# Sorting the tokens of a mixture of experts by expert group into 19 tiles of eight experts

## The chip, the cores and the metric

The kernel runs on one core of one Trainium2 chip, as one launch. The metric is the device time of that launch in microseconds, from timed executions; one further execution was profiled. The engines named below are PE (the matrix engine TensorE), VectorE (DVE), ScalarE (ACT), GpSimd (POOL) and SyncE (SP), which issues most DMAs.

## What is computed

The input is x, 4 sequences of 1024 tokens of 256 numbers. Two blocks follow one another, each `x + attention(norm(x)) * silu(ffn(norm(x)))`. The change touches the first block. Its FFN, cut to what matters:

```python
sb = sigmoid(x @ gate_w.T) + gate_bias                # 32 experts in 4 groups of 8
_, gidx = top_k(sum of the two best of each group, 2) # 2 groups of each token
_, topi = top_k(masked to these two groups, 8)        # 8 experts of 16
cw[token, topi] = wsel / wsel.sum() * 2.5             # weights, zero elsewhere
x_lat = x @ fc1_w.T                                   # 256 -> 128
h = relu(einsum('tl,eil->eti', x_lat, w1)) ** 2       # 128 -> 128 per expert
y_lat = einsum('eti,eli->tl', h * cw, w2)             # 128 -> 128, summed over experts
out = relu(x @ shared_up_w.T) ** 2 @ shared_down_w.T + y_lat @ fc2_w.T
```

The attention beside it has 16 heads of 16 and LoRA-extended projections; its q, k and v are computed in the same stage as the FFN.

## The kernel before

The 4096 tokens are cut into 8 chunks of 512 (`CH`). The kernel has four stages, each with its own blocks of instructions for the five engines: `first_half` (norm, q, k, v, the whole FFN of block 1), `first_attention`, `gate_network` (the FFN of block 2) and the second attention. Within a stage each engine walks through one list of steps, made by `first_half_plan` or `first_attention_plan`, and does its own part of each. So the list sets the order of the work on every engine, SP's DMA issues among them, and each engine is strictly in order. `Psum` hands out the eight banks of PSUM to the steps: PE waits in `P.all_before(s)` until the bank's last user is through.

In `first_half` a chunk goes through these steps. `load` and `sums`, `begin`: x is loaded and normed. `turn`: PE turns it, ScalarE writes the high part `xh`, VectorE the low part `xl`; products of such pairs are three products (`mm3`, lines 104 to 109). `gate`, `gate_turn`, `latent`: scores and the 128 latent numbers of a token. `groups`, `chosen`, `eight`, `weigh`: VectorE picks groups and experts with some fifty small instructions and writes the weights `cw`. `qk`, `values`, `shared`: projections; q, k, v are stored to DRAM (`qk_rest`, `values` on SP). Then all 32 experts on all 512 tokens: `up` (PE, three products of 512 columns; ScalarE: relu in line 490, square into `sq` in line 496), `down` (PE, line 596, two passes for each of four groups of 128 tokens), and VectorE adds the product times `cw[:, i, e]` to the sum `y` (line 797). The tail of a chunk is `tail_turn` (the sum is turned), `mix` (shared `sdn` and routed `fc2` products into one bank) and a sigmoid and product that leave silu(ffn) in `M["g"]`. It runs while the next chunk's experts do. While the experts of chunk c run, the steps of chunk c+1 up to `shared` are slipped in between.

Near the end `ahead` loads the q and k of the first two units of the attention, and 19 `max` steps (`BEGUN`) are done ahead: two score products of 512 columns in a pair of banks, and one VectorE reduction over both (line 176). 13 of them stand between the experts of the last chunk, six between the parts of its tail. `rows` turns the finished maxima, and `store_rows` writes them by four DMAs into the rows that the first score product reads.

In `first_attention` a step pair is one `max`, one pair of score products (line 1043), two exponentials on ScalarE (line 1007) and the product with the values (line 1056, `pv`). 256 steps `i` with two halves each make up the stage. The `max` steps keep ahead of the scores and take two pairs of banks in turn. `weights` steps (`GATE`) quantize the weights of the next stage.

Of the kernel before, what the change touches and what calls it, by code (L numbers as in the profile page):

```python
# [10 lines left out]
ALU = mybir.AluOpType  # L11
# [14 lines left out]
ACT_TURNS = (0, 1, 2, 3)  # L26
# [191 lines left out]

def first_half_plan():

    p = [("load", 0), ("weights",), ("load", 1), ("sums", 0), ("begin", 0), ("w_first",)]
    p += [("w_lora", n, k) for n in range(4) for k in range(2)]
    p += [("turn", 0, 0), ("turn", 0, 1), ("gate", 0), ("latent", 0), ("gate_turn", 0), ("groups", 0),
          ("w_shared",), ("w_experts", 0), ("shared", 0, 0), ("chosen", 0), ("shared", 0, 1), ("eight", 0),
          ("shared", 0, 2), ("weigh", 0), ("shared", 0, 3), ("qk", 0, 0), ("qk", 0, 1), ("qk_rest", 0, 0)]
    begun = {0: [("values", 0, 0)], 1: [("qk_rest", 0, 1), ("qk", 0, 2)], 2: [("values", 0, 1), ("w_experts", 1)],
             3: [("qk_rest", 0, 2), ("qk", 0, 3)], 5: [("qk_rest", 0, 3)], 10: [("w_experts", 2)],
             18: [("w_experts", 3)]}
    plan = {0: [("sums",)], 2: [("begin",)], 4: [("turn", 0)], 5: [("turn", 1)], 6: [("gate",)], 7: [("latent",)],
            8: [("gate_turn",)], 9: [("groups",)], 10: [("qk", 0)], 12: [("qk_rest", 0), ("chosen",)],  # L230
            13: [("qk", 1)], 15: [("qk_rest", 1), ("eight",)], 16: [("qk", 2)], 18: [("qk_rest", 2), ("weigh",)],
            19: [("qk", 3)], 20: [("values", 0)], 21: [("qk_rest", 3)], 22: [("shared", 0)], 24: [("shared", 1)],
            26: [("shared", 2)], 28: [("values", 1)], 30: [("shared", 3)]}

    begin = range(7, E, 2)
    tail = {1: [("tail_turn",)], 3: [("mix", 0)], 5: [("mix", 1)]}
    for c in range(NCH):
        if c + 2 < NCH:
            p.append(("load", c + 2))
        p += [("up", c, 0), ("up", c, 1)]  # L240
        for e in range(E):
            if c:
                p += [(s[0], c - 1, *s[1:]) for s in tail.get(e, [])]
                if c == NCH - 1 and e in (6, 16):
                    p.append(("ahead", e // 16))
            else:
                p += begun.get(e, [])
            if c + 1 < NCH:
                p += [(s[0], c + 1, *s[1:]) for s in plan.get(e, [])]
            if e + 2 < E:  # L250
                p.append(("up", c, e + 2))
            if c == NCH - 1 and e in begin:
                p.append(("max", begin.index(e)))
            p.append(("down", c, e))
    last = NCH - 1

    def maximum(n):
        x = len(begin) + n
        return [("max", x), ("both", 0)] if x == 15 else [("max", x)]

    p += [("mix_up", last, 0, 0)] + maximum(0)
    p += [("tail_turn", last)] + maximum(1)
    p += [("mix_up", last, 0, 1), ("mix_end", last, 0)] + maximum(2)
    p += [("mix", last, 0), ("mix_up", last, 1, 0)] + maximum(3)
    p += [("rows", 0)] + maximum(4)
    p += [("mix_up", last, 1, 1)] + maximum(5)
    return p + [("mix_end", last, 1), ("mix", last, 1)]

def first_half(nc, block, A, M, X):  # L270
    with ExitStack() as ctx:
# [7 lines left out]
        xh = [M["xh"][:, :, i * CH:(i + 1) * CH] for i in range(2)]  # L279
        xl = [M["xl"][:, :, i * CH:(i + 1) * CH] for i in range(2)]  # L280
        aa = [sb(f"aa{i}", [128, 2, CH], FR) for i in range(2)]
        va = sb("va_", [128, 2, H0, 32])
        lh = [sb(f"xlh{i}", [128, CH], FR) for i in range(2)]
        ll = [sb(f"xll{i}", [128, CH], FR) for i in range(2)]
        scT = sb("scT", [E, CH])
        sc = sb("sc", [128, 4, E])
        cw = [sb(f"cw{i}", [128, 4, E]) for i in range(2)]
        g = {k: sb(k, s) for k, s in dict(
            sb_=[128, 4, E], m8=[128, 16, 8], gs=[128, 4, 4], cc=[128, 4, 6], wn=[128, 4, 4], sel=[128, 4, 4],
            nb=[128, 4, 4], mk=[128, 4, E], mk2=[128, 4, E], t8=[128, 4, 8], rp=[128, 4, E], tk=[128, 4, E],  # L290
            ww=[128, 4, E], sm=[128, 4], rc=[128, 4]).items()}
        rl = M["rl"]
        sq = [sb(f"sq{i}", [128, CH]) for i in range(4)]
        hs = [sb(f"hs{i}", [128, 4, CH]) for i in range(2)]
        y = [sb(f"yac{i}", [128, 4, 128]) for i in range(2)]
        yT = sb("yT", [128, CH])
        sg = sb("sg", [128, 2, 256])
        bk = sb("bk", [128, 2, 2])
        x_t = A["x"].rearrange("(c i p) d -> c p i d", i=4, p=128)

        lora = hs[1]
        r_qkv = [t[:, :, :].rearrange("p a b -> p (a b)").rearrange("p (c o) -> p c o", c=2) for t in y]
        r_qkv.append(sq[3][:, :].rearrange("p (c o) -> p c o", c=2))
        r_f = yT[:, 0:320].rearrange("p (c o) -> p c o", c=2)
        r_s = hs[0][:, 0:2, :]
        r_1 = [hs[i][:, j:j + 2, :].rearrange("p a b -> p (a b)").rearrange("p (e o) -> p e o", e=8)
               for i, j in ((0, 2), (1, 0), (1, 2), (1, 0))]
        folded = r_qkv + [M["wo"]]

        plan = first_half_plan()
        P = M["banks"].stage()
        small = n_max = 0
# [1887 lines left out]
```

## Time and profile before

| | us |
|---|---|
| timed executions, median of 3 | 3142.89 |
| lowest, highest | 3141.05, 3150.26 |
| the profiled execution, its own time | 3153.16 |
| its span, first to last instruction | 3151.3 |

| busy in the profiled span | us | share |
|---|---|---|
| PE | 3018.0 | 96% |
| VectorE | 2118.1 | 67% |
| ScalarE | 1862.7 | 59% |
| GpSimd | 1013.5 | 32% |

The profile gives for each engine its busy time; for groups of instructions their number, busy time and mean duration; and for idle time of an engine what ended it. PE's matmuls overlap: the duration of one is longer than the distance to the next, so the distance between two starts is what one costs. A matmul of plain float32 appears as two. The clock that PE was granted is either full (1.0) or half (0.5) in any stretch. The first score product of the attention starts at 678.85 us, and the attention's last product at 1457.25 us.

### The profile page before, as it was taken

Reading aid. Unit: us, or ns where it says so; the run is one execution under the profiler, and the core shown is the slowest. Engines: PE = TensorE matmul, PEld = TensorE weight load, DVE = VectorE, ACT = ScalarE, POOL = GpSimd, SP = SyncE. Lnnn points to the kernel's source line nnn. Section 1 sums busy time; section 2 is a strip of 40 time slices with the busy share of each in tenths; the row PEclk is TensorE's granted clock in tenths of the full one; section 3 lists DMA queues with packets and bytes.
Section 4 is the critical chain, followed back from the end, with each engine's and each line's share of the span. In section 5 each row is a group of like instructions: output and inputs, shape, how many; then the busy total and the mean of one; then the engine's idle time right before and its main releaser. Section 6 shows DMA issues by size and latency. Waiting matters only on the chain. (4 is left out here: it accounts for less than half of the span.)

```text
span 3151.3 us, 66387 instructions
## 1 busy us (share of the span) xinstructions
PE 3018.0 (96%) x23638; PEld 2264.8 (72%) x23638; DVE 2118.1 (67%) x5888; ACT 1862.7 (59%) x4638; POOL 1013.5 (32%) x1627
## 2 busy tenths in 40 slices
PE   7999999999999999997988999999999999999999
PEld 5888888853444444444877888788887888788887
DVE  5666666678999989984755555655556555565556
ACT  4666666647877777774445555455554555545553
POOL 0000000001100000001016566576655766566653
PEclk9999999988999999998999999999999999999999
DMA  4111111231332232202324434354343543344431
GB/s 150 48 48 48 48 48 41 61 69 31 81 48 55 46 73 35 42 4 89 115 59 111 104 94 99 96 128 103 84 117 87 119 103 93 93 115 110 97 89 44
DMA packets 296483, 246.35 MB, mean 78 GB/s; under 512 B 148956, under 2 KB 231516, under 8 KB 296028
## 3 DMA queue, kind: packets, MB, share of 16 engines
q1 hardware_dynamic: 296156, 242.11, 31.2%
q8 instruction: 191, 3.13, 0.4%
q14 instruction: 136, 1.11, 0.1%
HBM read 100.71 MB, written 44.04 MB: 46 GB/s over the span
## 5 line engine op out<-in xcount | busy, mean ns | idle before, releaser
L1853 ACT ACTIVATE b_pp<-b_pp,b_nm 128x192 f32<-128x192 f32 (+2 forms) x1024 | 472.9, 463 | 452.8 <-DVE b_nm L2020 371.3
L176 DVE TENSOR_REDUCE mx<-ps 128x2 f32<-128x1024 f32 x512 | 622.4, 1224 | 64.4 <-PE ps L167 51.9
L1007 ACT ACTIVATE a_pt<-ps 128x512 f32<-128x512 f32 x1024 | 555.9, 595 | 185.3 <-PE ps L1043 184.3
L1823 POOL TENSOR_SCALAR b_pp<-b_pp,b_rc 128x192 f32<-128x192 f32 x960 | 387.0, 425 | 384.8 <-DVE b_rc L2029 384.8
L2041 DVE COPY b_pt<-ps 128x384 f32<-128x384 f32 (+2 forms) x336 | 181.9, 555 | 317.1 <-PE ps L1942 301.8
L2020 DVE CUSTOM_DVE_ANT_0 b_pp<-ps,b_mk 128x192 f32<-128x192 f32 x960 | 276.3, 353 | 134.9 <-PE ps L1921 134.9
L797 DVE SCALAR_TENSOR_TENSOR f_yac<-ps,f_cw,f_yac 128x128 f32<-128x128 f32 x992 | 277.9, 343 | 125.4 <-PE ps L596 123.0
L596 PEld LDWEIGHTS ps<-w,f_sq 128*128 128x128 f32 x2048 | 265.1, 191 | 26.5 <-issue 6.0
L596 PE MATMUL ps<-w,f_sq 128*128 128x128 f32 x2048 | 270.1, 275 | 0.3
L1976 PE MATMUL ps<-b_wo,b_oT 128*128 128x256 f32 x1024 | 241.6, 380 | 3.7 <-ACT b_vv L1846 3.7
L1056 PE MATMUL ps<-a_pt,a_v 128*32 128x256 f32 x3072 | 242.9, 396 | 0.0
L1942 PE MATMUL ps<-ident,b_pp 128*128 128x128 f32 x1440 | 234.2, 273 | 2.7 <-DVE b_qp L1998 2.5
L990 POOL TENSOR_TENSOR a_s<-a_s,g 128x256 f32<-128x256 f32 x32 | 23.4, 730 | 573.9 <-DVE a_s L1114 573.9
L1921 PE MATMUL ps<-b_kp,b_qp 64*128 64x192 f32 x1920 | 189.9, 337 | 18.0 <-ACT b_vv L1846 10.2
L1976 PEld LDWEIGHTS ps<-b_wo,b_oT 128*128 128x128 f32 x1024 | 185.3, 190 | 25.3 <-ACT b_vv L1846 4.4
L1942 PEld LDWEIGHTS ps<-ident,b_pp 128*128 128x128 f32 x1440 | 177.8, 141 | 34.2 <-issue 3.7
L490 ACT ACTIVATE rl<-ps 128x512 f32<-128x512 f32 x256 | 151.7, 593 | 80.0 <-PE ps L109 75.5
L1846 ACT ACTIVATE b_vv<-ps 128x256 f32<-128x256 f32 x256 | 97.5, 381 | 169.1 <-PE ps L109 168.8
L1921 PEld LDWEIGHTS ps<-b_kp,b_qp 64*128 64x128 f32 x1920 | 154.7, 188 | 56.3 <-issue 56.3
L1995 DVE TENSOR_TENSOR b_qf<-ps,xt 128x512 f32<-128x512 f32 x256 | 174.2, 681 | 29.5 <-PE ps L109 29.5
L1853 ACT ACTIVATION_READ_ACCUMULATOR b_pp<-b_pp,b_nm 128x1 f32 x1024 | 191.3, 187 | 0.0
L1968 PE MATMUL ps<-b_pt,b_vv 128*64 128x128 f32 x960 | 189.6, 279 | 0.0
(282 smaller groups left out, 7335.9 us busy)
## 6 DMA issues: line engine op xcount, KB each, us to landing
b_rt<-b_qf SPq DMA_DIRECT2D x1024, 64.0 KB, 2.0
qk_parts<-f_aa SPq DMA_DIRECT2D x32, 512.0 KB, 2.7
v_rows<-f_va_ SPq DMA_DIRECT2D x16, 512.0 KB, 2.8
rl<-in_W1qT SPq DMA_DIRECT2D x64, 128.0 KB, 2.6
rl<-in_W1kT SPq DMA_DIRECT2D x64, 128.0 KB, 2.6
rl<-in_W1vT SPq DMA_DIRECT2D x32, 256.0 KB, 3.0
b_wo<-in_W1oT SPq DMA_DIRECT2D x16, 512.0 KB, 3.7
b_vs<-b_vv SPq DMA_DIRECT2D x60, 128.0 KB, 2.9
```

What stands on the lines that cost most here:

```text
L176: e.tensor_reduce(M["mx"][kh % 3][:, :, jt, h], P.pair(s), AX.X, ALU.max, negate=True).then_inc(P.free_sem(s), 1)
L596: m = e.matmul(P.ap(s)[:, i * 128:(i + 1) * 128], sq[d % 4][:, i * 128:(i + 1) * 128], M["w2"][:, s[2], :], start=True, stop=True)
L797: m = e.scalar_tensor_tensor(out=o, in0=src, scalar=by, in1=o, op0=ALU.mult, op1=ALU.add)
L1007: e.activation(pt[(4 * i + 2 * j + a) % 12][:, :], P.ap((*s, a)), ACT.Exp).then_inc(P.free_sem((*s, a)), 1)
L1056: m = e.matmul(P.ap(group)[32 * j:32 * j + 32, x], vs[b % 2][c][:, 4 * g + j, :], pt[(4 * i + j) % 12][:, x], start=c == half == 0, stop=c ...
L1823: m = e.tensor_scalar(x, x, r[:, 2 * u + h:2 * u + h + 1], 1.0, ALU.mult, ALU.mult)
L1853: e.activation(x, x, ACT.Exp, bias=nm[n % 4][:, c:c + 1], scale=-1.0, accum_out=sm[n % 4][:, c:c + 1]).then_inc(exp_done, 1)
L1921: m = e.matmul(scores(u, h), q[r, d:d + 128], kk[r, d:d + 192], start=True, stop=True)
L1942: m = e.transpose(P.ap(f)[:, c * 128:(c + 1) * 128], pp[n % 3][:, at:at + 128], ident[:, :])
L1968: e.matmul(o1, v[:, i + u, right + 64:right + 128], y[:, 2, :], start=u == 0, stop=False)
L1976: m = e.matmul(P.ap(s)[:, 0:256], oT[:, n % 2 * 4 + c, t * 128:(t + 1) * 128], wo[n % 2][:, c, :], start=c == 0, stop=c == 3)
L2020: m = e.tensor_tensor_reduce(out=weights(n, u, h), in0=scores(u, h), in1=mask, scale=-0.125, scalar=3e38, op0=ALU.add, op1=ALU.min, accum_ ...
```

## The change

Instead of running all 32 experts on all tokens, each token is copied once for each of its two groups into a slot of a table in DRAM, sorted by group; each group starts at a multiple of 512 slots. 8192 pairs of token and group then fill at most 19 tiles of 512 slots, and a tile is run through the eight experts of one group. Weights of a slot are those eight entries of `cw`, carried behind the 128 latent numbers (`SW` = 136).

- Phase one, eight chunks: `turn`, then four `row` steps, each one product of 128 tokens with v, fc1 and gate beside one another (416 columns). ScalarE takes sigmoid and latent copy from it, VectorE the values. `begin` moves from VectorE to GpSimd. The routing steps stay on VectorE and gain instructions that count (`one1`, `total`); `rank` counts with products of a triangular matrix the place of each token in its group. `qk`, `shared`, `sdn` are put into a list `behind` and dealt out as `quota`; up to six chunks of `xh`, `xl` are kept for this (`RING`).
- At the start SP writes zeros over the whole slot table, ahead of the load of chunk 1. The folds of v come before those of q, k and o.
- `places` computes the position of each pair and the group of each tile. 64 indirect DMAs on GpSimd (`scatter`) write the rows to their slots. 42 pieces of `behind` stand after it for PE.
- Phase two, 19 tiles: `w_load` loads the group's weights (1 MB, address from a register), `w_split` splits them (ScalarE, GpSimd), `slots` loads the rows, `lat` turns them, then `up` and `down` for eight experts, and `y_out` stores the sums. The maxima stand in the last four tiles (16) and behind them (3), all in one pair of banks.
- The routed tail moves into the attention, chunk c at steps 8c+8 to 8c+15: `gather` (eight indirect DMAs), `add`, `tail_turn`, `mix` (fc2, added to the shared part in `M["g"]`), `ex` (max, exp, +1) and `silu` (reciprocal on VectorE, product on GpSimd). The `weights` steps move from step 16 to step 84.
The diff, cut to its core:

```diff
 def first_half_plan():
-    p = [("load", 0), ("weights",), ("load", 1), ("sums", 0), ("begin", 0), ("w_first",)]
+    p = [("load", 0), ("weights",), ("load", 1), ("sums", 0), ("begin", 0)]
+    p += [("w_lora", 2, k) for k in range(2)] + [("w_first",), ("turn", 0, 0), ("turn", 0, 1), ("sums", 1), ("begin", 1)]
+    p += [("w_lora", n, k) for n in (0, 1) for k in range(2)]
...
+    c = NCH - 1
+    p += [("groups", c)] + quota(1) + [("chosen", c)] + quota(1) + [("eight", c)] + quota(1) + [("weigh", c)]
+    p += quota(1) + [("rank", c)] + quota(1) + [("places",)]
+    p += [("scatter", n) for n in range(32)] + [("w_load", m) for m in range(1)]
+    while behind:
+        p += quota(1)
+    p += [("slots", 0), ("w_split", 0), ("w_load", 1), ("slots", 1), ("lat", 0)]
+    for m in range(NT):
+        p += [("up", m, 0), ("up", m, 1)]
+        for e in range(NE):
+            if m + 1 < NT and e == 1:
+                p.append(("w_split", m + 1))
+            if m + 1 < NT and e == 3:
+                p.append(("lat", m + 1))
+            if e + 2 < NE:
+                p.append(("up", m, e + 2))
+            if m < 2 and e == 0:
+                p.append(("ahead", m))
+            if m >= NT - 4 and e % 2:
+                p.append(("max", (m - NT + 4) * 4 + e // 2))
...
+            p.append(("down", m, e))
+            if e == NE - 1:
+                p.append(("y_out", m))
+                if m + 2 < NT:
+                    p += [("w_load", m + 2), ("slots", m + 2)]
+    return p + [("max", 16), ("max", 17), ("rows", 0), ("max", 18)]
...
+                    for i in range(4):
+                        n = NT * GT // 4
+                        e.dma_start(X["slots"][i * n:(i + 1) * n, :].rearrange("(p r) d -> p r d", p=128),
+                                    spread(zero[:, :], 1, n // 128)).then_inc(zero_out, 16)
...
+                elif k == "w_load":
+                    w.wait_ge(pos_ready, 3)
+                    if c == 1:
+                        w.wait_ge(*P.filled(("sdn", NCH - 2, 1)))
+                    if c >= 2:
+                        w.wait_ge(*P.filled(("down", c - 2, NE - 1)))
+                    group = e.value_load(tile_of[0:1, c:c + 1], min_val=0, max_val=NG - 1)
+                    e.dma_start(raw[c % 2][:, :, :].rearrange("p e f -> p (e f)"),
+                                A["w12"][bass.ds(group, 1), :, :].rearrange("a p f -> p (a f)")).then_inc(raw_in[c % 2], 16)
...
+                elif k == "y_out":
+                    w.wait_ge(*P.emptied(("down", c, NE - 1)))
+                    e.dma_start(X["y"][c * GT:(c + 1) * GT, :].rearrange("(i p) d -> p i d", p=128),
+                                y[c % 2]).then_inc(y_out[c % 2], 16)
...
+                elif k == "scatter":
+                    w.wait_ge(picked, 2 * NCH)
+                    w.wait_ge(row_act, 4 * NCH)
+                    w.wait_ge(zero_out, 64)
+                    w.wait_ge(pos_ready, 2)
+                    for i in range(2):
+                        e.indirect_dma_start(X["slots"], bass.IndirectOffsetOnAxis(ap=M["pos"][:, i, c:c + 1], axis=0),
+                                             rows[:, c, i, :], None).then_inc(row_out, 16)
+                elif k == "w_split":
+                    w.wait_ge(e_high, c + 1)
+                    if c >= 2:
+                        w.wait_ge(*P.filled(("up", c - 2, NE - 1)))
+                    e.tensor_tensor(w1[1][c % 2], raw[c % 2][:, :, 0:128], w1[0][c % 2].bitcast(F32),
+                                    ALU.subtract).then_inc(e_low, 1)
...
+                elif k == "w_split":
+                    w.wait_ge(raw_in[c % 2], 16 * (c // 2 + 1))
...
+                    e.activation(w1[0][c % 2], raw[c % 2][:, :, 0:128], ACT.Copy).then_inc(e_high, 1)
...
+                elif k == "row":
...
+                    for j in range(2):
+                        m = mm3(e, P.ap(s)[:, 0:416], xh[c % RING][:, j, t], xl[c % RING][:, j, t],
+                                M["wr_h"][:, j, :], M["wr_l"][:, j, :], j == 0, j == 1)
+                    m.then_inc(P.full_sem(s), 1)
...
 def first_attention_plan():
...
+        if 8 <= i < 8 * NCH + 8:
+            x, k = i // 8 - 1, i % 8
+            if k == 0:
+                p.append(("add", x))
+                if x + 1 < NCH:
+                    p.append(("gather", x + 1))
+            elif k == 2:
+                p.append(("tail_turn", x))
+            elif k in (3, 4):
+                p.append(("mix", x, k - 3))
+            elif k == 5:
+                p += [("ex", x, y) for y in range(2)]
+            elif k == 7:
+                p += [("silu", x, y) for y in range(2)]
...
+                elif k == "silu":
+                    w.wait_ge(up_one, 2 * s[1] + n + 1)
+                    e.reciprocal(ex[n], ex[n]).then_inc(inverted, 1)
```

## Rows read from the trace of the kernel before

**Rows 1.** Cores: span and mean granted clock; page, part 1: busy time.

```profile
core 0: 3151.3 us, clock 0.985
PE 3018.0 (96%) x23638; PEld 2264.8 (72%) x23638; DVE 2118.1 (67%) x5888; ACT 1862.7 (59%) x4638; POOL 1013.5 (32%) x1627
```

**Rows 2.** Timeline of PE in chunk 1: start, duration, engine, line, operation, count.

```profile
204.71 0.60 PE L602 MATMUL ps<-ident,f_yac 128*128 128x128 f32 x4
205.06 0.48 PE L107 MATMUL ps<-f_xlh,w_h 128*128 128x512 f32 x1
...
206.65 0.48 PE L107 MATMUL ps<-f_xlh,w_h 128*128 128x512 f32 x1
...
208.33 1.89 PE L534 MATMUL ps<-sdn,f_hs 128*128 128x256 f32 x8
210.06 0.59 PE L539 MATMUL ps<-fc,f_yT 128*128 128x256 f32 x2
```

**Rows 3.** Timeline of PE: first gate product, and two products of 256 columns.

```profile
27.00 0.77 PE L107 MATMUL ps<-xh,wg_h 128*128 128x512 f32 x1 [1.61 <-DVE xl L693]
...
49.29 0.28 PE L107 MATMUL ps<-wqkv_h,xh 128*128 128x256 f32 x1
49.41 0.28 PE L108 MATMUL ps<-wqkv_l,xh 128*128 128x256 f32 x1
```

**Rows 4.** DMA issues, size and time to landing, of 14:16, 22:32, and the page.

```profile
xt<-in_x SPq DMA_DIRECT2D x1, 512.0 KB, 11.8
...
f_hs<-in_w1T SPq DMA_DIRECT2D x2, 512.0 KB, 4.5
...
b_rt<-b_qf SPq DMA_DIRECT2D x1024, 64.0 KB, 2.0
```

**Rows 5.** Groups by line (busy, mean ns, idle before); last, an SP issue.

```profile
L496 ACT ACTIVATE f_sq<-rl 128x512 f32<-128x512 f32 x250 | 158.0, 632 | 8.0
L490 ACT ACTIVATE rl<-ps 128x512 f32<-128x512 f32 x251 | 148.7, 593 | 78.8 <-PE ps L109 74.3
...
L434 ACT ACTIVATE w1b_h<-f_hs 128x1024 fp32r<-128x1024 f32 x2 | 2.1, 1042 | 0.0
...
L990 POOL TENSOR_TENSOR a_s<-a_s,g 128x256 f32<-128x256 f32 x32 | 23.4, 730 | 573.9 <-DVE a_s L1114 573.9
...
0.74 0.44 SPq L362 DMA_DIRECT2D xt<-in_x  x1
```

**Rows 6.** Timeline of PE at the crossing into the attention.

```profile
678.85 0.49 PE L1043 MATMUL ps<-xh,xl 50*128 50x512 f32 x2 [0.96 <-DMA xh<-n]
681.46 0.79 PE L1043 MATMUL ps<-xh,xl 50*128 50x512 f32 x2 [2.11 <-ACT a_pt L1007]
```

**Rows 7.** Busy time by stretch: PE, PEld, DVE, ACT, POOL, granted clock, DMA.

```profile
678.85:732.00 53.15, 50.05 (x269) 17.44 (x269) 32.91 (x30) 27.66 (x50) 0.29 (x3) 0.52 0.22 51
732.00:784.00 52.00, 48.38 (x449) 20.88 (x449) 47.44 (x47) 41.95 (x78) 11.33 (x5) 0.99 0.24 46
```

**Rows 8.** Groups by line and form: VectorE's reciprocals.

```profile
L2029 DVE RECIPROCAL b_rc<-b_sm 128x8 f32<-128x8 f32 x120 | 23.0, 192 | 0.0
...
L1101 DVE RECIPROCAL a_rc<-ps 128x16 f32<-128x16 f32 x32 | 8.2, 257 | 20.2 <-PE ps L1066 19.7
...
L2029 DVE RECIPROCAL b_rc<-b_sm 128x2 f32<-128x2 f32 x32 | 5.0, 155 | 0.2 <-ACT b_pp L1853 0.2
```

**Rows 9.** Page, part 5: the maxima on VectorE.

```profile
L176 DVE TENSOR_REDUCE mx<-ps 128x2 f32<-128x1024 f32 x512 | 622.4, 1224 | 64.4 <-PE ps L167 51.9
```

**Rows 10.** Timeline of PE in the attention around a second low spell.

```profile
782.84 0.50 PE L167 MATMUL ps<-w1b_l,w1b_h 48*128 48x512 f32 x2 [0.85 <-DVE mx L176]
...
784.66 0.79 PE L167 MATMUL ps<-w1b_l,w1b_h 48*128 48x512 f32 x2
...
786.79 0.50 PE L167 MATMUL ps<-w1b_l,w1b_h 48*128 48x512 f32 x2
...
788.03 0.50 PE L167 MATMUL ps<-w1b_l,w1b_h 48*128 48x512 f32 x2
```

More of the change, by code:

```diff
@@ L25 @@
 NTURN = B * NP
-ACT_TURNS = (0, 1, 2, 3)
+GT, SW = 512, 136
 class Waits:
@@ L216, in store_rows @@
                         M["n2"][n % 2][8 * a:8 * a + 8, r, :].bitcast(F32)).then_inc(M["rows_in"][i][h], 16)
+NG = 4
+NT = 19
+NE = E // NG
+RING = 6
 def first_half_plan():
-    p = [("load", 0), ("weights",), ("load", 1), ("sums", 0), ("begin", 0), ("w_first",)]
[L222 to L233, printed above, removed]
@@ L238, in first_half_plan, with quota @@
+    behind += [[("sdn", NCH - 1, j // 2, j % 2)] for j in range(4)]
+    def quota(n):
+        out = []
+        for s in behind[:n]:
+            out += s
+        del behind[:n]
+        return out
+    for c in range(NCH):
+        if c:
+            p += [("turn", c, 0), ("turn", c, 1)]
         if c + 2 < NCH:
             p.append(("load", c + 2))
[L240 to L267, printed above, removed]
+        if c and c + 1 < NCH:
+            p += [("sums", c + 1), ("begin", c + 1)]
@@ new lines, in first_half_plan @@
+        if c == 0:
+            p += [("row", 0, 0), ("row", 0, 1), ("val", 0, 0), ("row", 0, 2), ("val", 0, 1), ("row", 0, 3),
+                  ("val", 0, 2), ("w_shared",), ("val", 0, 3)]
+            p += [("w_lora", 3, k) for k in range(2)]
+            continue
+        p += [("groups", c - 1)] + quota(1)
+        p += [("row", c, 0), ("chosen", c - 1), ("row", c, 1), ("val", c, 0)] + quota(1)
+        p += [("eight", c - 1), ("row", c, 2), ("val", c, 1)] + quota(1)
+        p += [("weigh", c - 1), ("row", c, 3), ("val", c, 2)] + quota(1)
@@ L312, in first_half @@
         P = M["banks"].stage()
-        small = n_max = 0
-        in_chunk = sum(s[0] == "max" for s in plan[:plan.index(("down", NCH - 1, E - 1))])
+        n_small = n_b = n_max = 0
+        begun = sum(s[0] == "max" for s in plan)
         for s in plan:
             if s[0] == "max":
-                x = 6 * (n_max % 2) if s[1] >= in_chunk else 0
-                P.take(s, x, x + 1)
-                n_max += 1
-            elif s[0] == "rows":
-                P.take(s, 4)
-            elif s[0] == "mix_up":
-                if s[3] == 0:
-                    P.take(("mix", *s[1:3]), 2 + s[2])
-            elif s[0] in ("tail_turn", "mix") and s[1] == NCH - 1:
-                if s[0] == "tail_turn":
-                    P.take(s, 5)
-            elif s[0] in ("w_lora", "turn", "gate", "gate_turn", "latent", "qk", "values", "shared", "tail_turn", "mix"):
-                P.take(s, small % 3)
-                small += 1
+                P.take(s, 0, 1)
+            elif s[0] in ("w_lora", "turn", "row", "rank"):
+                P.take(s, n_small % 4)
+                n_small += 1
+            elif s[0] == "places":
+                P.take(s, n_small % 4)
+                n_small += 1
+            elif s[0] in ("qk", "shared"):
+                P.take(s, 4 + n_b % 3)
+                n_b += 1
+            elif s[0] == "sdn" and s[3] == 0:
+                P.take(("sdn", *s[1:3]), 7)
+            elif s[0] in ("lat", "rows"):
+                P.take(s, 2)
@@ L346, in first_half @@
         y_done, dve_done = sem("y"), sem("dve")
-        LOW = {"gate": 1, "latent": 2, "bias": 3, "q": 5, "k": 7, "v": 9, "shared": 10, "experts": 11}
+        LOW = {"v": 2, "f": 3, "g": 4, "bias": 5, "q": 7, "k": 9, "shared": 10}
         def x_is_used(c):
-            return P.filled(("shared", c, 3) if c else ("qk", 0, 3))
+            return P.filled(last_use[c])
         def sync(e):
@@ L903, in first_attention @@
                 last = 0
-            elif s[0] in ("rows", "one", "two", "three") or s[:2] == ("weights", "sum"):
+            elif s[0] in ("rows", "one", "two", "three", "tail_turn", "mix") or s[:2] == ("weights", "sum"):
                 if last is None:
```

642 lines of the change are left out of this document (397 added, 245 removed).

## The prediction

> **What bounds the kernel now.** I read the page first. PE is busy for 96% of the span and the granted clock is 0.985 on average [rows 1]: time goes down only if PE has less to do, and goes up wherever PE is made to wait. Then the PE timeline inside a chunk of the first half [rows 2]. One expert on 512 tokens is a pitch of 1.59 us (205.06 to 206.65), three products of 512 columns and eight narrow passes, with no idle between. The reader is to see that this pitch stands 256 times (8 chunks x 32 experts), 407 us of the 679 us before the attention [rows 6]. Last, the attention: PE 48.4 and VectorE 47.4 busy of 52 us [rows 7]. Two engines are nearly full there, and a double maximum keeps VectorE for 1.23 us [rows 9].
>
> **Experts.** 19 tiles x 8 experts replace 256 units by 152: 104 x 1.59 = 165.4 us less of PE, all on the path. This is the only large gain.
>
> **Token rows.** Gate, latent and values (12 products of 512 columns and 24 of 256 a chunk; one of 256 takes 0.12 us [rows 3], so one of 512 some 0.23; with four small turns 5.8 us) become 24 products of 416 columns at 0.19 us, 4.5 us. Eight chunks: -9 us. The routed tail (four turns in 0.35 us; four fc2 products, of the form of the four sdn products that have a pitch of 1.73 us; 2.1 us a chunk [rows 2]) leaves the first half: -17 us here; its return is priced below.
>
> **Tile overhead.** 19 `lat` turns at 0.35 us, and 19 starts instead of 8 where PE waits some 0.25 us for the first square: +10 us.
>
> **Start.** The zero fill of the slot tensor (9728 rows of 544 B, 5.3 MB, four DMAs) is put on SP ahead of the load of chunk 1. Before, that load, issued between 14 and 16 us, landed 11.8 us later [rows 4], behind some 3.9 MB; 4.3 MB in 12 to 15.5 us is 0.28 to 0.36 MB/us. Now 7 MB lie there (the 2.5 MB of expert weights are gone): 20 to 25 us, landing near 36 us. VectorE has `sums` 1 ahead of the folds of q and k, those hold the small banks, and `row` 0 wants them: PE waits for this load. First token product near 39 us instead of 27.00 us [rows 3]; the earlier fold of v buys nothing. Since less PE work lies ahead of that point than before, I take +9 us; bounds -10 (the fill does not delay the load) to +15.
>
> **Scatter.** After `places`, PE has 42 pieces of `behind` left: 12 qk and 13 shared at 1.4 us, 17 sdn at 1.73 us [rows 2], 64 us. Against this stand about 3 us of small VectorE steps, 64 indirect DMAs on POOL, a landing of 2.0 us [rows 4], the load of `slots` (2.8 us), turns and splits (2 us). The trace shows no indirect DMA. Below: the issue of a plain one, 0.44 us [rows 5], 28 us in all, hidden. Above: each waiting for its own landing, 2.0 us, 128 us, 74 exposed. I take the sum of that issue and one 0.73 us POOL pass [rows 5], 1.2 us: 77 us, so 23 us exposed, and 3 us for a clock that then starts low: +26 us, bounds 0 to +77.
> The Trainium skill (DMA: Bandwidth & Descriptors, Anatomy of one DMA, SWDGE path) calls descriptor generation small and lays the 2 us on the completion; by it the scatter would be hidden and the sum 26 us lower. No row here shows it.
>
> **Weights of a tile.** `w_load` m+2 stands on SP behind `y_out` m, which waits for VectorE's last accumulation of tile m (1.35 us after its last product T). With the issue, a register load and the next issue it leaves at T+2.7; 1 MB was two 512 KB loads landing in 4.5 us [rows 4]: T+7.3. ScalarE meets its `w_split` in the next tile after three expert units, at T+4.2, and blocks. Behind it stand a copy of 1024 columns (1.04 us) and five units of 1.23 us (0.593 + 0.632) with the `lat` copy [rows 5]: the last `down` ends 9 us after the landing, T+16.4, where PE alone needs 13.1. That is 3.3 us for 14 tiles and 1 us for the three that also hold maxima: +49 us, bounds 25 (landing 1.4 us sooner) to 60. Each tile then has a hole of 2.6 us; if the clock falls in it, up to 2.6 us more a tile; I take 10 us, bounds 0 to 44. The split's POOL part (about 2.6 us) is hidden in the rest of the tile, and so are the slot loads. Cover gone, each costs its length.
>
> **Crossing to the attention.** Before, PE idled 0.96 and 2.11 us there and the clock fell [rows 6]. Now only four maxima and a turn lie between the last `down` and the first score, which waits for `rows` and its four DMAs: about +3.5 us. The 19 maxima themselves are the same number.
>
> **The tail inside the attention.** Per chunk PE gets 2.1 us, POOL and ScalarE short steps and eight gathers, which their idle time hides. VectorE gets two PSUM adds (1.4 us) and two reciprocals of 128x512. Reciprocals of 2, 8 and 16 columns took 155, 192 and 257 ns [rows 8]: 6.2 to 8.1 ns a column, not the one-a-cycle of a plain step. So 3.3 to 4.3 us each; I take 3.8, 7.6 us in one block. Only two maxima's banks lie ahead of PE, so PE stands about 6 us in each block. That is a hole larger than those after which the clock fell before: 0.85 us idle was followed by one short low spell, the crossing by one of about 51 us [rows 6, 10]. At the low level the pitch of the steps was 2.13 us (784.66 to 786.79), at the high one 1.24 [rows 10]. Per chunk: 6.2 (hole) + 2.1 + 6 (some seven slots at the low level, 0.89 us each) = 14.3, eight chunks: +114 us. Bounds: +55 (VectorE's 9 us a chunk less its 2 us slack, clock never lost) to +200 (low throughout: 16 x 0.89 + 4.2 + 6 a chunk).
> The Trainium skill (VectorE: DVE Perf Modes, First, the fixed hardware budget) says that reciprocal is an iterated divide with a repeat count of 8; at that page's 0.96 GHz that is, as an estimate, 4.3 us a tile and about 8 us more in all. The rows agree in kind.
>
> **Sum.** -165 - 9 - 17 + 10 + 9 + 26 + 49 + 10 + 3.5 + 114 = +30 us. The profiled execution took 3153.2 us (span 3151.3), the median of the timed runs is 3142.9; nothing after the first attention is touched, so the same 30 us go on the median: 3173 us.
>
> **Rivals.**
> 1. The clock comes back at once and the holes are all that is paid: tail +60 instead of +114, no low clock in the tiles. Then -34, 3109 us. For it: the spell at 783 us was short [rows 10]. Against: the 51 us spell came with PE fully busy [rows 7].
> 2. Reciprocals run near a column a cycle and the fixed part grows instead: tail +30, 3089 us. Against: three sizes in a line [rows 8].
> 3. Transfers are quicker than I say: scatter hidden, `w_load` in time: 26 + 59 less, 3088 us. It decides at 1 us an indirect DMA and a landing at T+4.2; the 4.5 us of [rows 4] speak against.
> 4. The clock stays low through the eight chunks: +200 instead of +114, 3259 us; it decides where holes recur sooner than the clock returns (hole each 30 to 40 us, spell 51 us).
> 5. The sort doesn't do what it says: 19 tiles hold any split of 8192 pairs into four groups, so the units are 152 whatever the data; this falls away.
>
> **How the numbers follow.** Forecast 0.42 (own range 3145 to 3215), rival 1 0.22, rival 2 0.08, rival 3 0.13, rival 4 0.15. Likeliest: 3173 us. Range for 8 in 10: 3075 to 3255. A measurement can tell about 0.3%, 9.4 us. Slower: 0.38 of the forecast, all of rival 4, little of rival 1: 0.56. Same: 0.10. Faster: 0.34.
>
> **What the profile would show.** `f_sq` products x1216 (two passes each of 608) instead of x2048. First token product near 39 us, else the start is wrong. The last scatter's end on POOL against the last sdn product; idle of PE there near 23 us. In tiles 1 to 17 a pitch of 16 us with an idle of ScalarE released by the raw load; 13 us if wrong. Reciprocals of 128x512 on VectorE at 3 to 4.5 us, each pair followed by an idle of PE put down to `mx`, and a granted clock well under 1 for the first eight half units of the attention. A reciprocal under 1 us or a clock at 1.0 there would make the prediction wrong by the most.

## The result, and the profile after

The kernel after took 3269.7 us (3263.9 to 3275.0), the kernel before 3142.0 us in the same job: a ratio of 1.040, 95% interval 1.037 to 1.044. It is slower, and 97 us over the 3173 us forecast. The unchanged kernel after was run in two more jobs (a job is one sitting on one chip, with runs of the kernel before between): 3264.7 us in one, 3201.5 us in the other, while the kernel before stayed at 3140 to 3143. So there are two numbers to explain: +59 us, which it cost in the second of these, and +64 us more, which it cost in the others.

The cores and part 1 of the page of the kernel after, which answer to [rows 1]:

```profile
core 0: 3273.2 us, clock 0.949
...
PE 2950.1 (90%) x22524; PEld 2154.9 (66%) x22524; DVE 2051.8 (63%) x5496; ACT 1767.8 (54%) x4528; POOL 1314.0 (40%) x1912
```

PE is busy 68 us less than before, and the span is 122 us longer: PE's idle time grew by 190 us. Where, is seen from three points. The last product of the last `down` starts at 664.6 us (before: 663.6), the first score at 674.9 (678.85, [rows 6]), the last one at 1557.8 (1441.4). Before the attention the kernel gained 4 us instead of the 84 of the sum; the attention grew by 120 us, where the sum had 114; behind it 5 us were added.

**The scatter.** Busy time by stretch (PE, PEld, DVE, ACT, POOL, granted clock, DMA), and below it ScalarE's timeline in the same stretch, then PE's and GpSimd's:

```profile
190.00:230.00 40.00, 18.95 (x82) 14.94 (x80) 3.12 (x5) 7.31 (x12) 30.05 (x32) 0.79 0.39 131
230.00:275.00 45.00, 12.58 (x34) 9.02 (x34) 0.75 (x1) 2.51 (x4) 31.54 (x33) 0.58 0.19 65
```

```profile
214.76 0.69 ACT L584 ACTIVATE f_aa<-ps,bqk 128x512 fp32r<-128x512 f32 x1 [5.83 <-remote]
233.66 0.60 ACT L600 ACTIVATE g<-ps 128x512 f32<-128x512 f32 x1 [18.21 <-remote]
250.46 0.60 ACT L590 ACTIVATE f_rl<-ps 128x512 f32<-128x512 f32 x1 [16.20 <-remote]
...
267.26 0.69 ACT L584 ACTIVATE f_aa<-ps,bqk 128x512 fp32r<-128x512 f32 x1 [15.54 <-issue]
280.61 0.60 ACT L590 ACTIVATE f_rl<-ps 128x512 f32<-128x512 f32 x1 [12.66 <-remote]
```

```profile
204.06 1.89 PE L706 MATMUL ps<-sdn,f_hs 128*128 128x256 f32 x8
...
251.86 3.75 PE L706 MATMUL ps<-sdn,f_hs 128*128 128x256 f32 x8 [41.87 <-issue]
```

```profile
205.94 0.96 POOL L535 DMA_INDIRECT slot_rows<-f_rows,pos  x1 [0.31 <-issue]
```

PE works for 31.5 of 85 us, though 64 us of pieces stand ready. ScalarE copies the sdn product of 204.06 only at 233.66, 28 us after PE's last pass of it, and its wait ends on a semaphore event ("remote") with no instruction near it. The trace also holds the moment of each increment: those of PE's banks come singly at 207.65, 214.74, 233.64 and 250.44, and then four within 0.25 us, from 280.59 to 280.83, seven us after the end of the last indirect DMA (273.5). The products were done, their increments were not out. (ScalarE's start at 267.26, 17 us after the one before, has no increment of PE beside it in the trace.) VectorE's and ScalarE's own increments came at once. GpSimd issues an indirect DMA every 1.26 us all that time.

**A tile.** SP's queue, then the wait that it ends on ScalarE and on PE, around 400 us:

```profile
395.45 0.35 SPq L453 DMA_DIRECT2D f_hs<-in_w  x1
395.85 0.43 SPq L460 DMA_DIRECT2D f_rows<-slot_rows  x1
```

```profile
401.45 1.06 ACT L608 ACTIVATE w1b_h<-f_hs 128x1024 fp32r<-128x1024 f32 x1 [4.01 <-DMA f_hs<-in_w]
```

```profile
402.27 0.66 PE L713 MATMUL ps<-ident,f_rows 128*128 128x128 f32 x4 [2.67 <-DMA f_rows<-slot_rows]
```

The weights land 6.0 us after their issue and ScalarE stands 4.0 us for them; PE stands 2.7 us at `lat`, for the slot load that was issued behind them.

**The attention.** VectorE, and PE behind it:

```profile
777.83 6.55 DVE L1308 RECIPROCAL a_raw<-a_raw 128x512 f32<-128x512 f32 x2
```

```profile
785.52 0.79 PE L167 MATMUL ps<-w1b_l,w1b_h 48*128 48x512 f32 x2 [4.99 <-DVE mx L176]
```

One reciprocal of 512 columns takes 3.3 us; each pair leaves PE idle for 5 us, and a spell of the low clock (783.5, for 20.5 us) begins in that hole. Behind the first spell of 51 us stand 13 more before the last score, 3 to 20 us long; in the kernel before, one of 3 us did.

### The profile page after: what moved, and what is told of

Read it like the earlier page. It is cut to its first block and busy times, and to the rows that moved or that the text cites. A ratio compares the mean times of both kernels' runs of the same rounds, so it can differ in the third digit from the quotient of the medians.

```text
span 3273.2 us, 63773 instructions
## 1 busy us (share of the span) xinstructions
PE 2950.1 (90%) x22524; PEld 2154.9 (66%) x22524; DVE 2051.8 (63%) x5496; ACT 1767.8 (54%) x4528; POOL 1314.0 (40%) x1912
## 5 line engine op out<-in xcount | busy, mean ns | idle before, releaser
L2184 PE MATMUL ps<-b_pt,b_vs 128*64 128x128 f32 x960 | 190.4, 280 | 0.0
L2186 PE MATMUL ps<-b_pt,b_vb 128*64 128x128 f32 x960 | 184.1, 274 | 0.0
L2187 PE MATMUL ps<-b_pt,b_vb 128*64 128x128 f32 x960 | 184.1, 274 | 0.0
L941 DVE SCALAR_TENSOR_TENSOR rl<-ps,f_rows,rl 128x128 f32<-128x128 f32 x532 | 147.3, 345 | 34.5 <-PE ps L724 34.1
```

What stands on the lines that cost most here:

```text
L2184: e.matmul(o0, vs[x][:, i + u, :], y[:, 0, :], start=u == 0, stop=False)
L2186: e.matmul(o0, vb[x][:, i + u, 0:64], y[:, 1, :], start=False, stop=u == 3)
```

## The experiments

The stages of every kernel, in us of its profiled execution; the first tile begins with its `lat`, and the pitch is an eighteenth of the time from there to the last product of the 19th `lat`. "Attention" runs from the first to the last score. The kernel before took 3140 to 3144 us in every job (median).

| kernel | job | first tile | pitch | first score | attention | time |
|---|---|---|---|---|---|---|
| before | | | | 678.9 | 762.5 | 3142 |
| after | 1 | 319.9 | 17.73 | 674.9 | 882.9 | 3269.7 |
| e1, plain passes | 2 | 284.0 | 17.43 | 633.5 | 869.6 | 3211.5 |
| e2, paced | 2 | 277.6 | 17.65 | 630.8 | 861.2 | 3202.9 |
| e3, three buffers | 2 | 278.6 | 14.14 | 567.5 | 848.6 | 3141.6 |
| e4, power on GpSimd | 2 | 278.6 | 17.61 | 631.9 | 2032.8 | 4377.8 |
| e5, after again | 3 | 278.4 | 17.08 | 621.6 | 860.4 | 3201.5 |
| e6, zero later | 3 | 259.5 | 17.36 | 607.6 | 865.2 | 3186.1 |
| e7, sigmoid | 3 | 278.5 | 17.59 | 631.1 | 842.5 | 3183.4 |
| e8, three fixes | 3 | 259.7 | 14.13 | 548.3 | 831.9 | 3097.6 |
| e9, no tail | 4 | 320.4 | 17.40 | 669.3 | 759.1 | 3146.2 |
| e10, exp and ln | 4 | 321.5 | 17.75 | 676.9 | 912.1 | 3295.1 |
| e11, three, ln | 4 | 302.6 | 14.28 | 593.9 | 908.4 | 3218.9 |
| e12, after, third | 4 | 321.6 | 17.55 | 673.3 | 869.1 | 3264.7 |
| e13, passes again | 5 | 282.8 | 17.24 | 629.2 | 878.8 | 3232.7 |
| e14, paced again | 5 | 287.7 | 17.81 | 644.1 | 881.3 | 3249.6 |
| e15, tanh | 5 | 321.1 | 17.41 | 670.2 | 844.4 | 3228.0 |
| e16, three, tanh | 5 | 301.8 | 14.14 | 590.6 | 842.6 | 3147.9 |
| e17, tanh, spread | 6 | 277.7 | 17.16 | 622.4 | 787.1 | 3125.0 |
| e18, all, paced | 6 | 259.3 | 14.12 | 547.8 | 784.1 | 3044.2 |

**What holds the increments back.** e1 and e13 put a plain pass in the place of each indirect DMA:

```diff
-                        e.indirect_dma_start(X["slots"], bass.IndirectOffsetOnAxis(ap=M["pos"][:, i, c:c + 1], axis=0),
-                                             rows[:, c, i, :], None).then_inc(row_out, 16)
+                        w.wait_ge(row_out, 16 * (2 * c + i))
+                        e.tensor_tensor(flat[:, 1024:1536], flat[:, 0:512], flat[:, 512:1024],
+                                        ALU.subtract).then_inc(row_out, 16)
```

> The 64 indirect DMAs of the scatter become 64 plain passes of 512 columns on GpSimd (about 1.3 us each, so GpSimd is busy as long as before); the rows are not put into the slot tensor, so the routed part of the output is left out. Theory A (the issue of indirect DMAs is what keeps TensorE's semaphore increments back): the 42 pieces run at their own pace between 190 and about 256 us, TensorE's idle there falls from over 50 us to about 20 (waiting for GpSimd at the end), the first tile starts near 282 instead of 318 us, time 30 to 40 us under the kernel after. Rival B (the stores of q and k, the 1 MB weight load or the sheer length of the GpSimd work stop ScalarE): the steps of about 17 us stay, less than 8 us gained.

PE's stall in the scatter was gone, but it was also gone from the three other kernels of that job, which kept their indirect DMAs. So e1 told nothing, and the kernel after had to be run again.

> The kernel after, unchanged, a second time. In its first trace TensorE stood 42 us between 209.6 and 251.9 us while its semaphore increments arrived in steps of about 17 us; four other kernels, one of which differs only inside the attention, issued the same 64 indirect DMAs without that stall, and their first tile started at 278 us against 320. Theory D (the stall belongs to this build and comes each time): 3262 to 3277 us again, the first tile near 320 us, increments in steps. Theory E (the stall was an event of that chip or of those executions): the first tile at 278 us and 3222 to 3238 us.

> The kernel after, unchanged, a third time, for how often its executions show the stall of 42 us in the scatter. Theory E (an event of single executions or one chip): first tile at 278 us and 3195 to 3225 us. Theory D (it belongs to the build): 3262 to 3277 us.

No stall in e5, the same stall in e12. The build is not its cause, and within a job it was there in every profiled execution with the 64 DMAs in a row, or in none. The test had to be made in a job that shows it, and job 5 did (e15: PE busy 19.2 us of the 40 from 190 to 230, first tile at 321.1; e16, whose scatter begins 18 us sooner: first tile at 301.8).

> The kernel of e1 (64 plain GpSimd passes of 512 columns in place of the 64 indirect DMAs; the routed part of the output is left out) a second time, beside kernels with the scatter in the same job. If the others of this job show the stall of 42 us (first tile near 320 us): theory A (it needs the indirect DMAs) gives a first tile at 284 us here and no held increments; theory B (it belongs to the chip or the rest of the program) a first tile near 320 us. If the others show no stall, this run decides nothing.

The stretches of e13, in that job:

```profile
190.00:230.00 40.00, 39.90 (x175) 32.79 (x176) 7.29 (x10) 18.31 (x29) 35.99 (x29) 1.00 0.40 142
230.00:275.00 45.00, 20.98 (x93) 16.89 (x91) 2.25 (x3) 10.32 (x16) 40.42 (x33) 0.79 0.10 38
```

GpSimd is busier than in the kernel after, the plain loads and stores are those of the kernel after, and PE never waits until its pieces end. The gathers in the attention, eight indirect DMAs in a row, are left in e13, and there PE does stand in the same execution, behind the row from 779.4 to 788.3 us for instance:

```profile
791.57 0.50 PE L167 MATMUL ps<-w1b_l,w1b_h 48*128 48x512 f32 x2 [2.56 <-ACT spare L1202]
```

Theory A holds: the stall needs the indirect DMAs. Whether their issue or their transfers hold the increments is not told apart, since e13 has neither. What differs between jobs stays open too; the five jobs of the experiments ran on five chips, so it can be the chip or the moment.

**Pacing them.** e2 and e14 put a `scatter` step behind each piece, and GpSimd waits for a product first:

```diff
+            p.append(("scatter", n, next((t for t in p[::-1] if t[0] in ("qk", "shared")))))
...
+                    w.wait_ge(*P.filled(s[2]))
```

> GpSimd issues two indirect DMAs and then waits for the next product of the pieces behind, instead of 64 in one go. Theory A with increments that pass as soon as GpSimd pauses: products and pairs interleave at about 2.5 us a pair, 32 pairs and the ten pieces left end near 290 to 295 us, so the tiles start 20 to 25 us sooner and the time is that much under the kernel after. Theory A' (each increment is held until some 6 us after GpSimd's last issue, as the burst of four at 280.6 us suggests): every pair costs about 9 us, 32 pairs 290 us, the time is 130 to 180 us over the kernel after. Rival B: no change within 8 us.

> The kernel of e2 (two indirect DMAs after each product of the pieces) a second time. In a job with the stall: theory A gives a first tile before 300 us if increments pass as soon as GpSimd waits, and far behind 320 us if each is held some 6 us after the last issue. In a job without it: 278 us as before.

In the quiet job it changed nothing at the first tile (277.6). In the job with the stall the first tile came at 287.7 instead of 321: theory A, not A'. The waits work only once PE is behind. From 190.8 to 223.6 us GpSimd still issued 26 in a row and PE stood once for 20.2 us; at its first pause, from 223.6 to 228.0, three increments came through. The time fell by less than the stage: 17 us under the mean of 3267 us for the kernel after in jobs 1 and 4, in another job.

**The tiles.**

```diff
-                if m + 2 < NT:
-                    p += [("w_load", m + 2), ("slots", m + 2)]
+                if m + 3 < NT:
+                    p += [("w_load", m + 3), ("slots", m + 3)]
```

(with a third buffer for each in the space of `rows`, and the waits and semaphores by 3).

> Three buffers instead of two for a tile's weights and for its slots, so that both loads leave a whole tile sooner. Theory (the tiles wait for these two loads): the pitch of a tile falls from 17.7 us to 13.7 to 14 us, the low clock in the tiles goes with it, 60 to 75 us under the kernel after. Rival (the split of the weights on ScalarE and GpSimd or VectorE's accumulation is late next): a pitch of 16 us or more, less than 30 us gained.

The pitch fell to 14.14 us, a little over the 13.7 to 14 expected: no wait of PE on a load is left between the first tile and the last. Its wait on VectorE's accumulation stays, this in each tile:

```profile
380.56 1.16 PE L727 MATMUL ps<-f_raw,f_rows 128*128 128x128 f32 x8 [0.33 <-DVE rl L944]
```

So VectorE is next, but for 0.3 us. From first tile to last `down` it is 278.5 us instead of the 332.9 us of e5: 54 us. The time fell by 60 us against e5, another job, and by 61 us against e2 in its own. Both loads were moved at once, so what the weights and what the slots cost is not told apart.

**The start.**

```diff
+        if 1 <= c <= 4:
+            p.append(("zero", c - 1))
...
+                elif k == "zero":
                     w.wait_ge(pool_set, 1)
-                    for i in range(4):
+                    for i in (c,):
```

> The four DMAs that zero the slot tensor leave the start and stand one each behind the loads of chunks 3 to 6. Theory (the load of chunk 1 waits behind the fill on the same rings): the first token product comes at 27 to 31 us instead of 40, and nothing else moves: 8 to 12 us under whatever the kernel after shows in the same job. Rival (the start waits for the weights and the folds, not for the fill): first token product at 38 us or later, less than 3 us.

The first token product in PE's timeline of e6:

```profile
21.37 0.72 PE L107 MATMUL ps<-wr_h,xh 128*128 128x416 f32 x1 [2.73 <-DVE f_rows L777]
```

That line stood at 39.48 us in e5, with an idle of 20.73 before it. The first tile came 18.9 us sooner, the time fell by 15 us, more than the 8 to 12 expected.

**The tail in the attention.** e9 leaves it out.

> The kernel after without the tail in the attention: gathers, sum, turns, fc2 products, exponential, reciprocal and product are left out (the routed part and the silu are missing from the output). Theory (the tail makes the attention longer, mostly through short holes after which the clock is low for 10 to 24 us): 762 us between first and last score as before, 85 to 100 us under the kernel after of the second job (3201 us). Rival (the low clock belongs to the changed state at the crossing, not to the tail): 820 us or more.

Busy time from the first to the last score of e9, columns as above:

```profile
669.30:1428.40 759.10, 720.02 (x6367) 311.43 (x6367) 653.88 (x690) 576.37 (x1058) 59.50 (x62) 0.97 0.26 48
```

759.1 us at a clock of 0.97, as before; e12 in the same job took 869.1. The tail costs 110 us there, all of it gone with it (the time is 118 us under that of e12). It remained to find which part. e4 moved the reciprocals to GpSimd:

```diff
-                    e.reciprocal(ex[n], ex[n]).then_inc(inverted, 1)
+                    e.tensor_tensor(ex[n].rearrange("p (a b) -> p a b", a=1), ex[n].rearrange("p (a b) -> p a b", a=1),
+                                    spread(neg[:, 0:1], 2, CH), ALU.pow).then_inc(inverted, 1)
```

> The two reciprocals of 128x512 a chunk go from VectorE to GpSimd (power of -1). Theory (the block of 6.6 us on VectorE and the clock that it costs make the attention long): TensorE's idles of 5 us put down to mx go, the granted clock is near 1 there, 75 to 105 us under the kernel after. Rival C (the eight indirect DMAs a chunk, the other thing that is new there, cause the holes): under 30 us gained, and idles of 3 us and low spells stay around each gather.

A miss: one power of 128x512 took 82 us on GpSimd, and it answers nothing. e7 used a sigmoid (`ACT.Sigmoid` in place of `ACT.Exp`, +1 and reciprocal dropped):

> Exponential, plus one and reciprocal of the tail are replaced by one sigmoid on ScalarE (two table loads of 1.28 us a chunk); VectorE has no reciprocal of 512 columns any more, and the rest of the tail stays. Theory (the 6.6 us block on VectorE makes the holes and takes the clock): the attention, 883 us in the kernel after and 762 us before, comes to 780 to 800 us, 70 to 100 us under the kernel after. Rival C (gathers, TensorE's added products, table loads): attention at 840 us or more.

ScalarE's timeline in one chunk of e7, between two exponentials:

```profile
748.71 1.28 ACT L1202 ACT_TABLE_LOAD   x1
750.00 1.15 ACT L1202 ACTIVATE a_raw<-a_raw 128x512 f32<-128x512 f32 x2
751.17 1.28 ACT L1192 ACT_TABLE_LOAD   x1
```

PE then waits 2.83 us for ScalarE in six of the eight chunks (1.7 and 2.2 us in the last two) in the place of 5 us for VectorE, spells of 10 to 24 us come back every 31 to 34 us, and only 18 us are gained. e10 took the logarithm:

```diff
+                    e.activation(ex[n], ex[n], ACT.Ln, bias=ones[:, 0:1]).then_inc(up_one, 1)
...
+                    e.activation(ex[n], ex[n], ACT.Exp, scale=-1.0).then_inc(inverted, 1)
```

> The reciprocal becomes three steps of ScalarE, exponential, logarithm and exponential, 0.6 us each and spread over four half steps; VectorE has none of it, and if logarithm and exponential share a table nothing is loaded. Theory (every hole of 2 to 5 us costs a low spell, wherever it comes from): no hole over 1 us in a chunk, spells of the sigmoid kernel gone, attention 785 to 800 us, 60 to 75 us under the kernel after. Rival (TensorE's added products or the indirect DMAs take the clock): attention at 830 us or more. If the table is loaded twice a chunk, as with the sigmoid: 830 to 845 us.

Four table loads a chunk: holes up to 3.5 us, attention 912 us, worse than the reciprocal (869.1 in e12, the same job). In the chunks of the attention the holes were followed by low spells whether VectorE had made them (5 us) or ScalarE (e7 and here, 1.7 to 3.5 us); the remedy failed. e15 took the tangent, `ACT.Tanh` of x/2 and one scale and add on GpSimd:

> The reciprocal goes by way of the hyperbolic tangent, x/2 (1 + tanh x/2), one step of 0.6 us on ScalarE. If it lies in the table that holds the exponential, there is no table load and no work on VectorE: no hole over 1 us in a chunk, few low spells, attention 775 to 800 us instead of 860 to 883. Rival (TensorE's own added products or the gathers take the clock): 830 us or more, as with the sigmoid and its table loads.

No table load, none of VectorE's reciprocals, and still 844 us. What is left are waits like this one in PE's timeline of e15, behind a chunk's row of eight gathers (770.4 to 779.2):

```profile
781.94 0.55 PE L1240 MATMUL ps<-w_h,w_l 50*128 50x512 f32 x2 [4.03 <-issue]
```

ScalarE's waits there end on "remote", as in the scatter (20.9 us of them from 700 to 1000). e17 gives each gather its own step:

```diff
-                if x + 1 < NCH:
-                    p.append(("gather", x + 1))
+            if x + 1 < NCH:
+                p.append(("gather", i, k, x + 1))
...
+                        w.wait_ge(*P.filled(("score", s[1], 0, 0)))
```

> The kernel of e15 with one change: the eight gathers of a chunk are issued one in each step of the attention, each behind that step's first score, instead of eight in a row. Theory A for the gathers (eight indirect DMAs in a row hold TensorE's increments for about 4 us, which is the hole that e15 still has in each chunk): in a job with the stall in the scatter (first tile near 320 us) the holes of 4 us and most low spells go, attention 785 to 800 us instead of 844; in a job without it the same length or less. Rival (the added products take the clock): 830 us or more.

Busy time from the first to the last score of e17:

```profile
622.40:1409.50 787.10, 747.39 (x6461) 324.66 (x6461) 663.66 (x706) 588.76 (x1082) 181.25 (x178) 0.96 0.28 51
```

787 us with the same added products and the same gathers: the rival falls, the holes were the cost. But this job showed no stall in the scatter, and the other traces say what that means. With eight gathers in a row PE stands for 1 to 4 us in or just behind some of the rows in every such kernel of jobs 1, 4 and 5. In none of those of jobs 2 and 3 (e1 to e8) is there, past the crossing, a hole over 0.7 us in such a place; what holes they have are those of the reciprocals or of the table loads. So the quiet job alone accounts for the missing holes of e17. What the spreading does in a job with the stall was not run.

**Together.** e8 joins e3, e6 and e7, e11 takes e10 instead of e7, e16 takes e15, e18 adds the pacing of both.

> The three together: three buffers for weights and slots, the zero fill later, the sigmoid. If they add up and the stall of the scatter does not come: 3272 less 42 (stall), less 64 (tiles), less 10 (start), less 85 (attention): about 3070 us, 2 to 2.5% under the kernel before. Rival (the gains share one cause, the clock, and do not add): 3110 us or more.

> Three buffers, the later zero fill and the exponential and logarithm together: 3098 us of the three with the sigmoid, less 35 to 50 us of the attention: 3050 to 3065 us, 2.5 to 3% under the kernel before. Rival: as the sigmoid version, 3090 us or more.

> Three buffers, the later zero fill and the tangent together: 3098 us less 30 to 55 us, 3043 to 3068 us in a job without the stall, 3085 to 3110 us in one with it. Rival (gains do not add): 3090 us or more without the stall.

> Three buffers, later zero fill, tangent, gathers spread and the scatter in pairs behind products. Theory A: in a job with the stall the tiles start near 270 us instead of 302 and the attention takes 785 to 800 us: 3065 to 3080 us, 2 to 2.5% under the kernel before; without the stall 3040 to 3055 us. Rival (held increments only move to other places): 3120 us or more in a job with the stall.

The core of e18:

```profile
core 0: 3044.5 us, clock 0.980
```

The gains of e8 add up: 104 us on e5 in the same job, where e6 gave 15, e7 18 and e3 60 against e5, 93 in all. e11 missed its range by the stall (first tile at 302.6 instead of 259.7) and by the table loads. e16 had a range for a job with the stall, 3085 to 3110 us, and missed it by 38 us: the attention took 842.6 us, with the holes behind its gathers. e18 takes 3044.2 us, inside its range, 0.967 of the kernel before (0.965 to 0.970): the sorted form is the faster one once these waits are gone. It was measured in a job without the stall; how much pacing saves it in one with the stall was not run.

## Why the prediction was wrong

The sign was right, the size was not, and most of the miss is one step. In spans the kernel after is 122 us over the kernel before where +30 was forecast. Of the 92 us between, 76 are what e5, without the stall, did not have (42 in the scatter, 12 in the tiles, 22 in the attention) and 27 with smaller terms before the attention; 5 came behind it, and the attention of e5 was 16 us shorter than forecast. By terms of the sum:

- **Experts, -165.** 152 units instead of 256. In e3 PE's timeline shows the pitch of 1.59 us again (first product of an `up` at 388.35, 389.95 and 391.54), eight to a tile. Right.
- **Token rows, -9 and -17.** The products of 416 columns have the pitch of 0.19 us that was taken (43.78 to 43.97 in e5). By the sum's own figures, 5.8 less 4.5 us in eight chunks, the first part is -10.
- **Tile overhead, +10.** In e3, where no load is waited for, the tiles without maxima follow each other at 14.04 us, where 13.1 was put into the sum. Eight experts are 12.7 and the turn is 0.35; the other 0.97 us lies at the seam between two tiles, where PE has three `down` in a row and then three `up`, and waits 0.33 us for VectorE and some 0.25 for the first square. 0.25 was priced: 19 times 0.7, some 14 us short.
- **Scatter, +26.** The issue of one was put at 1.2 us and is 0.96 us at a pitch of 1.26; in e5 PE stands 24 us at the end of its pieces instead of the 23 of the sum. Right in e5, a job without the stall. The failing step is the overlap: the sum let 64 us of pieces run on PE beside the scatter, and cover was taken as free of the thing it covers. In the measured job the pieces could not hand over, and the first tile came 42 us later (319.9 against 278.4 in e5). With that stall come 22 us in the attention between the two executions, where eight gathers in a row do the same on a small scale, and 12 us in the tiles, for which no cause is shown; the three make up the difference between the two spans. The bound of +77 would have held this term (26 and 42), not the sum: with 77 in it the forecast is 3224 us, 46 us short.
- By the Trainium skill (DMA: Bandwidth & Descriptors, Anatomy of one DMA, SWDGE path) the scatter would have been hidden. The trace does not agree: from the first of the 64 to the end of the last GpSimd was busy for 83 us, against 64 us of pieces, and in e5 PE stood 24 us at their end.
- **Start, +9.** The first token product was forecast near 39 us and came at 40.0 (before: 27.00, [rows 3]). The product came 13 us later where the sum had 9. What the fill costs is more, 18 us (e6); without it the earlier fold of v does pay: 21.4 us against 27.0.
- **Weights of a tile, +49 and +10.** Measured 54 us (e5 against e3). The size was right, one reason was not: that the slot loads are hidden is wrong: PE of the kernel after stood 40 us over 17 tiles for them, at the same time as ScalarE for the weights. The clock took little of it: in e5 four of these 17 holes are followed by a low spell, of 3.4 us each.
- **Crossing, +3.5.** PE is idle for 6.9 of the 10.4 us from the last `down` to the first score in e5, before for 1.6 of 15.3: 5.3 us.
- **Left out, 8.** The `rank` step puts ten narrow products on PE, 1.03 us a chunk (100.08 to 101.11 us), 8 us in all. No part of the sum priced it. These 8, the 14 of the seams, 4 of the start and 2 of the crossing, less 5 of the weights, are 23 of the 27 us by which e5 gains less before the attention (57) than forecast (84). The other 4 are not traced.
- **Tail, +114.** 98 in e5, where no hole stands behind the gathers; 120 in the kernel after, 110 from e9 and e12, with the holes behind the gathers in them. That 120 lies so near 114 is in part luck: the tail without the stall was put 16 us too high, and 22 us came from what the sum did not have. The reciprocal is 3.3 us where 3.8 was taken, PE stands 5.0 us where 6.2 was, and the spells are as forecast: one behind each pair of reciprocals, 10 to 20 us. Rival 2 (cheap reciprocals), rival 1 (the clock comes back at once) and rival 4 (it stays low throughout) are out. By the Trainium skill (VectorE: DVE Perf Modes, First, the fixed hardware budget) a tile was, as an estimate, 4.3 us. The trace has 3.3 us; the lower end of what the rows of 2 to 16 columns gave was nearer.
- **Rival 3** (transfers quicker) is out: the weights of a tile landed after 5.1 us in the median of the page and 6.0 in the tile shown, where 4.5 was read from [rows 4].

In e5 the kernel after took 3201 us, within the range (3075 to 3255) and the forecast's own (3145 to 3215). In two of three jobs it took 3265 to 3270, outside both.

## What to carry to other kernels

Price cover by what it needs from others: a piece of work hides something only if its hand-overs go through while that something runs. In the attention the holes of 1.7 to 5 us that the reciprocals (e5) and the sigmoid's table loads (e7) made were followed by 10 to 24 us at the low clock, and a hole of 5 us cost some 10 (in e5: 98 us less 17 of the tail's own products, by eight); in the tiles of e5 holes of 1.6 to 3.4 us were followed by 3.4 us of it or by none, so read the price off the stretch in question. Where a short step on a nearly full engine costs that much, take it off that engine, and look first at what it brings along where it goes (a table load, a row of indirect DMAs). When two runs of one kernel in different jobs differ by far more than each varies, run it again beside the experiments before reading a cause into either.
